# One stationary operand for the last 48 rows of the MoE up projections, and a layer-norm chain that runs in token halves

## The reference

```python
x = x + 0.5 * ffn0(layernorm(x))      # silu(x W1) * (x W3), Hadamard, W2; hidden 1024
x = x + mamba(layernorm(x))           # selective state space, inner 512, state 16
x = x + 0.5 * ffn0(layernorm(x))
x = x + 0.5 * moe(layernorm(x))
x = x + attention(layernorm(x))       # 16 heads, causal, ALiBi
x = x + 0.5 * moe(layernorm(x))       # the same weights as above
```

```python
scores = sigmoid(xt @ gate_w.T); top 2 of 8, normalised, times 2.5 -> combine
h = einsum('td,edh->eth', xt, w1); u = einsum('td,edh->eth', xt, w3)
y = einsum('eth,ehd->etd', silu(h) * u, w2)
out = einsum('etd,te->td', y, combine) + silu(xt @ sw1) * (xt @ sw3) @ sw2
```

## Time and profile before

| what | us |
|---|---|
| three runs, median (lowest to highest) | 850.93 (850.23 to 853.95) |
| the profiled execution: time | 852.66 |
| its span, first to last instruction | 850.7 |
| PE busy | 763.7 (90%) |
| DVE busy | 561.1 (66%) |
| ACT busy | 407.7 (48%) |
| POOL busy | 254.3 (30%) |
| mean granted PE clock | 0.967 |

### The profile page before, as it was taken

How to read it: one execution, slowest core, us unless ns; L and a number is a source line. 1 busy time by engine, 2 the same in 40 slices (tenths; PEclk the granted TensorE clock), 3 DMA queues, 4 the chain that set the end, 5 groups by cost and what they waited for, 6 DMA issues and landing times.

```text
span 850.7 us, 10806 instructions
## 1 busy us (share of the span) xinstructions
PE 763.7 (90%) x3862; PEld 527.4 (62%) x3862; DVE 561.1 (66%) x984; ACT 407.7 (48%) x600; POOL 254.3 (30%) x189
## 2 busy tenths in 40 slices
PE   4899989986779799999999998997899998788997
PEld 3587565653326366667876776774457775445776
DVE  4444699999969999963464446358765646844443
ACT  3344797666456787732232233441575421373221
POOL 0000059985428787850994000001000010000000
PEclk9999989999988999999998999999999999899999
DMA  9300022222101222217001000033000340000000
GB/s 279 115 2 1 2 62 75 74 75 62 50 26 56 64 71 65 79 38 229 2 1 22 1 1 0 13 110 94 10 1 1 80 115 30 2 27 1 1 1 25
DMA packets 30591, 41.75 MB, mean 49 GB/s; under 512 B 3753, under 2 KB 19955, under 8 KB 30515
## 3 DMA queue, kind: packets, MB, share of 16 engines
q1 hardware_dynamic: 29290, 40.91, 16.4%
q10 hardware_dynamic: 1252, 0.19, 0.2%
HBM read 36.73 MB, written 4.26 MB: 48 GB/s over the span
## 4 chain that ended last, share of the span: by engine, by line
PE 66%; DVE 15%; issue 9%; ACT 6%; DMA 2%; POOL 1%; SPq 0%; DVEq 0%; ACTq 0%
PE PS L495 35%; PE PS L835 7%; PE PS L573 3%; DVE PS L1938 3%; PE PS L1040 2%; PE PS L1023 2%; PE PS L801 2%; DVE shared L1946 2%; PE PS L616 2%; PE PS L722 1%; ACT shared L1547 1%; PE PS L453 1%; PE PS L819 1%; PE PS L904 1%; DMA shared<-in_L_ffn_W_dram 1%
## 5 line engine op out<-in xcount | busy, mean ns | idle before, releaser
L2254 POOL TENSOR_TENSOR shared<-shared,route 128x1024 f32<-128x1024 f32 x64 | 151.5, 2370 | 78.0 <-DVE shared L1946 72.3
L495 PE MATMUL PS<-xnT,work_r 128*128 128x512 f32 (+1 forms) x624 | 156.7, 402 | 0.0
L495 PE MATMUL PS<-xnT,weights_r 128*128 128x256 f32 (+1 forms) x732 | 155.3, 359 | 0.5 <-issue 0.4
L1946 DVE TENSOR_TENSOR_SCAN shared<-shared,PS 128x512 f32<-128x512 f32 x128 | 148.7, 1204 | 0.0
L495 PEld LDWEIGHTS PS<-xnT,weights_r 128*128 128x128 f32 x732 | 114.9, 191 | 33.3 <-issue 20.0
L495 PEld LDWEIGHTS PS<-xnT,work_r 128*128 128x128 f32 (+1 forms) x624 | 114.1, 188 | 28.7 <-issue 1.5
L835 PE MATMUL PS<-shared,cf 128*128 128x512 f32 x256 | 123.1, 604 | 0.0
L1705 DVE TENSOR_TENSOR gated<-gated,PS 128x512 f32<-128x512 f32 (+1 forms) x52 | 35.6, 685 | 106.4 <-ACT gated L1205 106.4
L1205 ACT ACTIVATE gated<-PS 128x512 f32<-128x512 f32 (+1 forms) x52 | 31.1, 598 | 143.8 <-PE PS L495 138.9
L1489 ACT ACTIVATE shared<-shared,cols 128x512 f32<-128x512 f32 x128 | 83.7, 712 | 24.2 <-DVE shared L1946 20.5
L495 PE MATMUL PS<-weights_r,work_r 128*128 128x256 f32 (+1 forms) x624 | 89.4, 293 | 1.4 <-DVE work_r L1712 1.1
(11 more groups left out here) (222 smaller groups left out, 1092.2 us busy)
## 6 DMA issues: line engine op xcount, KB each, us to landing
route<-scratch_c SPq DMA_DIRECT2D x64, 256.0 KB, 3.2
shared<-in_L_ffn_W_dram SPq DMA_DIRECT2D x3, 1024.0 KB, 8.9
scratch_k<-shared SPq DMA_DIRECT2D x12, 128.0 KB
scratch_q<-shared SPq DMA_DIRECT2D x12, 128.0 KB
shared<-scratch_k SPq DMA_DIRECT2D x8, 192.0 KB
shared<-scratch_q SPq DMA_DIRECT2D x8, 192.0 KB
mamba_w<-in_L_ffn_w_dram SPq DMA_DIRECT2D x2, 704.0 KB, 5.2
beside<-in_L_ffn_w_dram SPq DMA_DIRECT2D x2, 704.0 KB, 7.5
```

The lines of the kernel that those rows point to most:

```text
L495: last = nc.tensor.matmul(o, lhs[l], rhs[r], start=(start and i == 0), stop=(stop and i == 2))
L1946: v.tensor_tensor_scan(hst[:, (t % 2 * 2 + j) * T:(t % 2 * 2 + j + 1) * T], decay[t % D_SLOTS][:, j * T:(j + 1) * T], products[:, j * T:(j ...
L2254: nc.gpsimd.tensor_tensor(hc[:, u * 2 * T:(u + 1) * 2 * T].rearrange("p (c t) -> p c t", c=2), hst[:, (t % 2) * 2 * T:(t % 2 + 1) * 2 * T] ...
```

## The change

Five parts.

1. The 48 rows of the last chunk get one stationary operand for w1 and w3 together (`pair`, 112 columns: the 48 of w3, 16 that fill, the 48 of w1). `pair_product` issues six matmuls into bank 1: rows 0 to 47 are the w3 product, rows 64 to 111 the w1 product. ACT and DVE read the two parts of that bank. POOL's `halve_up` for this chunk has eight operations on 48 or 64 columns instead of four on 2x48.
2. At the three places `residual_statistics` replaces `residual` and the start of `norm_statistics`: the first 256 tokens are added and their statistics taken when the first half of the stage's last output product is there (new semaphore `half_down`), then the other 256.
3. At the same places `half_transposes` replaces the transposes: PE transposes the token chunks 0 and 1 of both feature chunks after the first two scalings (new semaphore `xn_half`), and the chunks 2 and 3 after `xn_done`.
4. In the attention part for batch 0 the statistics of batch 1 move from behind the mask of head 9 to in front of the mask of head 6.
5. `START_PRODUCTS` 8 to 4, `TAIL_PRODUCTS` (13, 18) to (8, 12).

A store of ones that nothing reads (`ones_row`) goes, and `pair_words` takes its place in memory.

The diff, cut to its core:

```diff
-START_PRODUCTS, TAIL_PRODUCTS = 8, (13, 18)
+START_PRODUCTS, TAIL_PRODUCTS = 4, (8, 12)
...
+            def half_transposes(self, k, n, banks):
+                pe = self.pe
+                for half in range(2):
+                    if half:
+                        pe.wait_ge(xn_done, k)
+                    else:
+                        pe.wait_ge(xn_half, n + 1)
+                    for ch in range(DC):
+                        for tc in (2 * half, 2 * half + 1):
+                            last = nc.tensor.transpose(bank(banks[ch])[:, tc * P:(tc + 1) * P],
+                                                       xn_tok[:, tc * D + ch * P:tc * D + (ch + 1) * P], ident[:, :])
+                        if half:
+                            last.then_inc(xnT_tr, 1)
...
+            def pair_product(self, o, b):
+                for k in range(DC):
+                    x_ = bass.ds(b * DC * T + k * T, T)
+                    last = self.product(o, pair[k], (xnT_hi[:, x_], xnT_lo[:, x_]), k == 0, k == DC - 1)
+                return last
...
-                        self.input_product(bank(p % 2)[0:rows, :], w1h, m * P, rows, MH, b)
-                        self.input_product(bank(2 + p % 2)[0:rows, :], w3h, m * P, rows, MH, b)\
-                            .then_inc(s["up"], 1)
+                        if m == MM - 1:
+                            self.pair_product(bank(p % 2)[0:PAIR_ROWS, :], b).then_inc(s["up"], 1)
+                        else:
+                            self.input_product(bank(p % 2), w1h, m * P, P, UP_COLS, b)
+                            self.input_product(bank(2 + p % 2), w3h, m * P, P, UP_COLS, b).then_inc(s["up"], 1)
...
-                nc.scalar.activation(gated[0:rows, slot * T:(slot + 1) * T], bank(slot)[0:rows, :], ACT.Silu)\
-                    .then_inc(s["silu"], 1)
+                o = bank(slot)[0:rows, :] if rows == P else bank(slot)[PAIR_AT:PAIR_ROWS, :]
+                nc.scalar.activation(gated[0:rows, slot * T:(slot + 1) * T], o, ACT.Silu).then_inc(s["silu"], 1)
...
+            def residual_statistics(self, it, b, scale, banks, n):
+                dve, rows = self.dve, self.rows_of_x(b)
+                r = [x_tok[:, (b * TC + 2 * h) * D:(b * TC + 2 * h + 2) * D] for h in range(2)]
+                nc.vector.memset(stats[:, 44:45], 0.0)
+                dve.wait_ge(half_down, n + 1)
+                self.link(nc.vector.scalar_tensor_tensor(r[0], bank(banks[0]), scale, r[0], ALU.mult, ALU.add))
+                for tc in (0, 1):
+                    nc.vector.bn_stats(stats[:, tc * 6:(tc + 1) * 6], rows[tc])
+                dve.wait_ge(down_done, it + 1)
+                nc.vector.scalar_tensor_tensor(r[1], bank(banks[1]), scale, r[1], ALU.mult, ALU.add)\
+                    .then_inc(resid_done, 1)
+                dve.wait_ge(resid_done, HEAD + it + 1)
+                for tc in (2, 3):
+                    last = nc.vector.bn_stats(stats[:, tc * 6:(tc + 1) * 6], rows[tc])
+                self.link(last)
+                self.aggregate()
...
+                if b == 0:
+                    self.norm_statistics(1)
+
                 def mask(h):
...
-                    if b == 0 and h == 9:
-                        self.norm_statistics(1)
```

More of the change, by code:

```diff
@@ L245, in build @@
         w2_lo, stacks_at = cut(weights_r, a, MM * D)
-        w1h, a = halves(UP_AT, DC * MH)
-        w3h, a = halves(a, DC * MH)
-        assert a == BESIDE_AT
+        w1h, a = halves(UP_AT, DC * UP_COLS)
+        w3h, a = halves(a, DC * UP_COLS)
+        pair_at = [work_r[:, a - WORK_AT + i * PAIR_ROWS:a - WORK_AT + (i + 1) * PAIR_ROWS] for i in range(3)]
+        assert a + 3 * PAIR_ROWS <= BESIDE_AT
+        pair = ((pair_at[0], pair_at[1]), (pair_at[2], pair_words[:, :]))
         raw = {}
@@ L575, in plain_chunk @@
                                             start=False, stop=(m == FM - 1 and tc % 2 == 1))
+                    if r == 0 and m == FM - 1 and tc == 1:
+                        last.then_inc(half_down, 1)
                 last.then_inc(s["used"] if m < FM - 1 else down_done, 1)
@@ L708, in moe @@
                 if (st, b) == (MOE1, 1):
-                    for ch in range(DC):
-                        self.norm_transpose(it + 1, ch, at=5 + ch)
+                    self.half_transposes(it + 1, 2, (5, 6))
                 if (st, b) == (MOE1, 1):
@@ L804, in mamba_output @@
                                             stop=(c == EC - 1 and tc % 2 == 1))
+                    if b == 1 and c == EC - 1 and tc == 1:
+                        last.then_inc(half_down, 1)
                 if c == EC - 1:
@@ L850, in mamba @@
                     self.idle_products(B_BANK, START_PRODUCTS)
-                    for ch in range(DC):
-                        self.norm_transpose(it + 1, ch, at=2 + ch)
+                    self.half_transposes(it + 1, 0, (2, 3))
                     for n in range(4, LEAD - 2):
@@ L958, in mamba @@
                     self.idle_products(B_BANK, TAIL_PRODUCTS[0])
-                    for ch in range(DC):
-                        self.norm_transpose(it + 3, ch, at=4 + ch)
+                    self.half_transposes(it + 3, 1, (4, 5))
             def attention(self, b):
@@ L1680, in norm_scale @@
                                                    ALU.subtract, ALU.mult)
+                    if halved and tc == 1:
+                        last.then_inc(xn_half, 1)
                 last.then_inc(xn_done, 1)
@@ L1704, in times_gate @@
                 self.dve.wait_ge(s["silu"], b * count + p + 1)
[L1705 removed]
+                return nc.vector.tensor_tensor(g, g, bank(2 + slot if rows == P else slot)[0:rows, :], ALU.mult)
             def low(self, s, b, count, p, rows=P):
@@ L2292, in halve_up @@
                 m = MOE_ORDER[p]
+                if m == MM - 1:
+                    pieces = []
+                    for k in range(DC):
+                        end = (k + 1) * MH
+                        pieces.append((w3s[:, end - LAST_ROWS:end], *(t[:, 0:LAST_ROWS] for t in pair[k])))
+                        pieces.append((w1s[:, end - PAIR_AT:end], *(t[:, LAST_ROWS:PAIR_ROWS] for t in pair[k])))
+                    halve(pieces).then_inc(moe_up, 1)
+                    return
                 def part(t):
-                    return t.rearrange("p (k h) -> p k h", k=DC)[:, :, m * P:m * P + rows_of_chunk(m)]
+                    return t.rearrange("p (k h) -> p k h", k=DC)[:, :, m * P:(m + 1) * P]
                 halve([(part(w), part(h[0]), part(h[1])) for w, h in ((w1s, w1h), (w3s, w3h))]).then_inc(moe_up, 1)
```

37 lines of the change are left out of this document (24 added, 13 removed).

## The result

The changed kernel took 846.85 us in the median of nine runs (842.55 to 848.49); the kernel before took 851.39 in nine runs beside them (849.64 to 854.82). The ratio is 0.9944 (95% interval 0.9925 to 0.9964): faster by 0.56%, or 4.5 us between the medians. The forecast was 7.4 us less and 843.8, with a range of 840.4 to 847.4. Its profiled execution took 847.64, with a span of 845.8, 4.9 under the span of before, at a mean granted clock of 0.968 (before 0.967).

The account below looks back on a forecast made before the run. PE was taken as the bound, with a DVE, ACT and PE chain at the places and DVE in pass 1. 4.23 + 2.69 + 0.44 = 7.36 off 850.93 gave 843.6, rounded to 843.8; range 840.4 to 847.4.

Parts of the forecast that it names:

- the clock takes back part of it: Rival: with shorter filling the first and second places fall to 1.2 GHz; gain only 4.0, time 846.9; chance 0.13.
- Joint stationary: MoE position 1: six matmuls fewer save 1.41 a pass in passes 2 to 4 (4.23), nothing in pass 1.
- Behind position 3 the PE runs its positions without a gap, so the gain is kept: MoE passes 2 to 4: what position 1 saves lasts to the end of the pass, 3 x 1.41 = 4.23.
- Statistics in halves: At the three places: adding and taking statistics by halves ends the last statistics 0.75 earlier, bounds 0.5 and 0.91.
- Transposes in halves: Second and third places: two transposes fewer before ACT's copy save 0.22 each; nothing at the first place.
- Masks, 0.44: Attention for batch 0: statistics moved into DVE's idle time shorten the span of the masks from 14.61 to 14.17.
- The idle stretches stay about as long or grow by 0.1 to 0.3: PE's idle time at the three places, since the filling shrinks by more than the chain before it.
- Cost nothing unless the clock falls: At the three places: fewer products on zeros block no transposes and cost nothing while the clock holds.
- more than forecast: Rival: the clock holds at the third place (1.7) and pass 1 also gains 1.41; gain 10.5, time 840.5; chance 0.12.
- Slower: Rival: new waits in pass 1 keep PE's clock low for over 30 us; time 856; chance 0.04.
- routing chain becomes the bound: Rival: routing chain or ACT bounds all MoE passes, so the joint stationary gives nothing; gain 3.1, time 847.8; chance 0.07.
- halves bring nothing: Rival: DVE pays in waits what the halves win; gain 4.7, time 846.2; counted inside the forecast's 0.64.

Follow-up runs that it names:

- experiment 7: The changed kernel with the six matmuls of the joint stationary issued twice; 848.16 in 12 runs, ratio 0.9968.
- experiment 6: The changed kernel with products on zeros added in the pause of each MoE pass (7 in pass 1, 3 in the others); 842.24, ratio 0.991.
- experiments 9 and 10: The changed kernel with `pair_words` 128 columns wide, not 112: 845.79; and the kernel before with `ones_row` 112 wide, not 128: 850.96 in one run.
- experiment 8: The changed kernel with the transposes at the three places in one piece again, the halved statistics kept; 846.11 in one run.
- experiment 3: The changed kernel with the old numbers of products on zeros (8, 13 and 18); 847.06 in 6 runs, ratio 0.9933.
- experiment 5: The changed kernel with no products on zeros at the three places; 850.57 in 12 runs, ratio 0.9997.

## Why the prediction was right, and where its sum was too high

The sign came out, and so did nearly every local term. The time, 846.85, lies in the range 840.4 to 847.4, but not in the 841.5 to 846.3 that the prediction gave its own mechanism. It lies on the 846.9 of the rival *the clock takes back part of it*, whose mechanism did not occur. So that the time fell in the range owes something to its width. The total came out at 4.5 in one set, 6.7 in the other and 6.3 at an equal clock, for a forecast of 7.36. The stages at equal clock loss add up to about 5.8 to 6.0: 2.81 to 2.89 at the places, 0.44 at the masks, 1.04 and 0.91 in passes 2 and 3, the same again taken for pass 4, less 0.24 in the feed-forward and 0.07 in pass 1.

- *Joint stationary, "6 x 0.235 = 1.41 a pass"*: right; 1.34 at the position, 1.38 to 1.39 over a pass (experiment 7). The Trainium skill (TensorE: Matmul & The Clock Gate, Part 3, The mechanism) lets a load overlap running matmuls only in other rows, in its list of what overlaps; the paragraph above that list also names a background weight buffer as a target for loads that go ahead. The trace differs from the list and fits the paragraph: the six matmuls with 112 columns took 1.48 in all, 0.247 each, and the six of experiment 7 added 0.231 each, no more than the 0.235 of those with 48, so no load shows as standing free. "In pass 1: gain 0" was too low: twice the matmuls cost 0.43 there.
- *"Behind position 3 the PE runs its positions without a gap, so the gain is kept"*: this is the step that failed. There is no gap, but the positions themselves became slower by 0.033, some ten of them a pass, and so did the products of the feed-forward (0.24). Pass 2 gained 77.99 - 76.95 = 1.04 (against experiment 6, both without clock loss), pass 3 0.91. The forecast priced what the edit computes and not where it moved the operands. Take 0.34 to 0.47 in each of passes 2 to 4 (the fourth could not be compared at equal loss), 0.24 in the feed-forward, and 0.50 in pass 1, which over all did not gain the 0.43 of experiment 7 but lost 0.07 (70.23 to 70.30 at equal loss). Then about 1.8 to 2.1 went this way. That the slower positions come from the place of the operands is shown (experiments 9 and 10), the size for the whole kernel is worked out from stages.
- *Statistics in halves, 0.75*: measured 0.67, 0.72 and 0.73. *Transposes in halves, 0.22 at two places*: 0.28 and 0.27, and 0.22 at the first place too. There "two chains end together" held only by the old order; in experiment 8 ACT is idle for 0.10 between its side copy and this one, which starts 0.70 behind the start of the side copy; in the changed kernel it is not idle, and that distance is 0.48. The places gave 0.89 + 1.00 + 1.00 = 2.89 (2.81 by PE's rows) for a forecast of 2.69.
- *Masks, 0.44*: 14.61 to 14.17, exact at the masks. Whether it reaches the end of the stage is not shown: from the second pass to the end of that attention part it took 57.4 to 58.6 in the seven profiles with one stretch at half clock there, two of which are without part 4.
- *POOL, "1.42 becomes 2.0 to 2.7"*: its operations for the last chunk went from 1.46 to 2.16 in all, and PE waited for none of them.
- *"The idle stretches stay about as long or grow by 0.1 to 0.3"*: wrong. They shrank, from 0.83 to 0.35, 0.85 to 0.55 and 1.57 to 1.41, since the first transposes start on half of `xn_tok`.
- *"Cost nothing unless the clock falls"*: right for the shortened filling (experiment 3), and the condition is real: with none it costs 3.5 (experiment 5).
- *The clock takes back part of it*: not at the first two places, where it was put; both kept 2.4 GHz. The half of *more than forecast* that concerned the third place came true in the profile, but in other stretches of the same execution the loss was larger, so the spans do not show it. What the rival got right is its size against the measurement: two stretches more or less of 1.7 are the scatter between the runs of one kernel.
- *Slower*, *routing chain becomes the bound*, *halves bring nothing*: none of them; between positions 1 and 3 of passes 2 to 4 PE has no wait but the pause of 0.83 to 0.88 that was there before.

The 1.8 between 4.5 and 6.3 stays within the scatter of nine and six runs.

The best version is the changed kernel with the filled pauses: 842.2 to 843.0 in three variants, 0.9 to 1.1% under the kernel before. Against the changed kernel that is 4 to 5 by the medians, but these come from different groups; by the ratios (mean 0.9902 of the three, 0.9933 of the changed kernel's two) it is 2.6, give or take 2.2. No two of the three can be told apart.

## What to carry to other kernels

Price an edit at its place, then measure the same work far from it: operands that moved, by as little as 64 bytes, took back about 2 us of the 7.4 that were forecast, in matmuls that the diff does not touch. Fill PE's pauses with products on zeros, but with few: having none at the three places cost 3.5 us here, and up to twice as many brought nothing. When the clock makes runs of one kernel differ by more than an edit is worth, compare stages of equal clock loss, and double the disputed work: 1.38 a pass could be read to 0.01 where the times could not tell 2 us.

## What was not expected of the hardware

- Matmuls of the same form at full clock ran 0.7% slower (4.720 to 4.753 us a position) after a displacement of 64 bytes in SBUF, and the effect does not add to that of another displacement. In the up products only the stationary operand had moved; for the down products it stays open which operand does it, and why is open for both.
- The granted clock was lost in steps: about 1.7 us of it in a stretch, or a multiple. The lost time is less where PE has a wait behind the stretch (1.65 for 3.4 in the second pass). In passes 3 and 4 most stretches stood behind pauses of only 0.83 to 0.88, and none came where these were filled; but the one that starts between 446 and 451 in pass 1 stood in all profiles, also where PE was never idle longer than 0.34 around it. What sets it was not found.
- One position of the mean clock's third decimal goes with about 0.45 us of time in the first group of runs, and this accounts for some six tenths of the variance within each kernel there.
